# Overflow rows of a mixture-of-experts layer in blocks of 128 instead of 256

## The reference

```python
def _L0_ffn_ref(x, W1, b1, W2, b2, W3, b3, Wg, bg):
    gate_logits = jnp.einsum('bsd,dn->bsn', x, Wg) + bg
    gate_weights = jax.nn.softmax(gate_logits, axis=-1)
    topv, topi = jax.lax.top_k(gate_weights, TOPK)      # TOPK = 2, NE = 8
    h = gelu(einsum('bsd,ndh->nbsh', x, W1) + b1)        # 512 -> 1024
    h = gelu(einsum('nbsh,nhf->nbsf', h, W2) + b2)       # 1024 -> 1024
    eo = einsum('nbsf,nfd->nbsd', h, W3) + b3            # 1024 -> 512
    comb = jnp.sum(jax.nn.one_hot(topi, NE, dtype=x.dtype) * topv[..., None], axis=-2)
    return jnp.einsum('nbsd,bsn->bsd', eo, comb)
x = x + _L0_xattn_ref(_layernorm(x), ctx_2048, ...)
x = x + _L0_ffn_ref(_layernorm(x), ...)
```

## Time and profile before

| | us |
|---|---|
| median of three runs | 876.22 |
| lowest, highest | 872.66, 877.42 |
| the profiled execution | 865.58 |
| its span, first to last instruction | 863.8 |
| start of the first block's transposes | 419.88 |
| start of the ninth block's first matmul | 802.73 |
| end of its last matmul | 849.80 |
| last busy instruction (a scatter) ends | 855.18 |

### The profile page before, as it was taken

How to read it: one execution, slowest core, us unless ns; L and a number is a source line. 1 busy time by engine, 2 the same in 40 slices (tenths; PEclk the granted TensorE clock), 3 DMA queues, 4 the chain that set the end, 5 groups by cost and what they waited for, 6 DMA issues and landing times.

```text
span 863.8 us, 17380 instructions
## 1 busy us (share of the span) xinstructions
PE 775.2 (90%) x5934; PEld 672.6 (78%) x5934; DVE 601.8 (70%) x1275; ACT 495.6 (57%) x1131; POOL 231.1 (27%) x286
## 2 busy tenths in 40 slices
PE   3889898989998999766499999999999999999993
PEld 2657676767776767444498999999999999999992
DVE  4476878787979787655575858676766757676863
ACT  4357777777777767685153645554545455464551
POOL 3232434343434343213460303030211203030300
PEclk9799999999999999775699999999999999999997
DMA  6641010202020100222795655556465565565540
GB/s 212 242 151 58 2 59 20 72 23 69 23 69 28 65 22 24 84 108 93 256 341 202 242 213 207 214 196 232 176 260 204 216 225 210 203 246 203 206 169 2
DMA packets 28209, 126.22 MB, mean 146 GB/s; under 512 B 4236, under 2 KB 4252, under 8 KB 17664
## 3 DMA queue, kind: packets, MB, share of 16 engines
q1 hardware_dynamic: 22544, 109.80, 35.6%
q0 software_dynamic: 5616, 15.81, 5.2%
HBM read 108.68 MB, written 19.01 MB: 148 GB/s over the span
## 4 chain that ended last, share of the span: by engine, by line
PE 67%; DVE 12%; ACT 8%; issue 5%; DMA 3%; POOL 3%; SPq 0%; POOLq 0%; ACTq 0%; DVEq 0%
PE tiles L1041 6%; PE tiles L1043 6%; PE tiles L1042 6%; PE scores L1304 4%; PE scores L1305 4%; PE scores L1303 4%; PE ptb L1151 4%; PE pvb L1043 3%; PE pvb L1042 3%; PE pvb L1041 3%; PE ptb L1043 3%; PE ptb L1042 3%; PE ptb L1041 3%; PE scores L1141 2%; PE pvb L1174 2%
## 5 line engine op out<-in xcount | busy, mean ns | idle before, releaser
L830 DVE TENSOR_TENSOR w<-scr,w 128x2048 fp32r<-128x2048 f32 x75 | 170.8, 2288 | 61.6 <-ACT w L620 61.6
L620 ACT ACTIVATE w<-scr 128x2048 fp32r<-128x2048 f32 x76 | 144.9, 1909 | 60.8 <-PE scores L1305 60.8
L473 POOL DMA_INDIRECT out_dram<-scr,tok x18 | 19.4, 1079 | 311.4 <-DVE scr L1027 308.7
L602 ACT ACTIVATE scr<-scr,rsum 112x257 f32<-112x257 f32 x128 | 66.5, 520 | 62.4 <-DVE rsum L814 62.4
L1041 PE MATMUL tiles<-c,w 128*128 128x256 f32 (+1 forms) x272 | 82.4, 303 | 18.3 <-DVE c L718 15.7
L1041 PE MATMUL tiles<-w 128*128 128x256 f32 x288 | 83.3, 289 | 0.9 <-DVE w L1017 0.2
L1015 DVE CAST w<-scr 128x256 fp32r<-128x256 f32 x144 | 43.8, 304 | 54.6 <-ACT scr L686 54.6
L1042 PE MATMUL tiles<-w 128*128 128x256 f32 x288 | 81.5, 283 | 0.0
L1043 PE MATMUL tiles<-w 128*128 128x256 f32 x288 | 81.4, 283 | 0.0
L1151 PE MATMUL ptb<-ident,scr 112*128 112x112 f32 x384 | 64.7, 280 | 18.3 <-ACT scr L610 16.6
L1042 PE MATMUL tiles<-c,w 128*128 128x256 f32 (+1 forms) x272 | 79.4, 292 | 0.0
(11 more groups left out here) (214 smaller groups left out, 2315.1 us busy)
## 6 DMA issues: line engine op xcount, KB each, us to landing
scr<-in_dram SPq DMA_DIRECT2D x82, 1024.0 KB, 4.8
scr<-in_dram SPq DMA_DIRECT2D x8, 750.0 KB, 4.5
scr<-slots_d SPq DMA_DIRECT2D x10, 528.0 KB, 5.5
slots_d<-rows SPq DMA_DIRECT2D x8, 528.0 KB, 11.6
xn<-in_dram SPq DMA_DIRECT2D x9, 256.0 KB
xb<-in_dram SPq DMA_DIRECT2D x8, 224.0 KB, 2.6
xr<-in_dram SPq DMA_DIRECT2D x8, 224.0 KB, 2.5
out_dram<-x SPq DMA_DIRECT2D x8, 224.0 KB, 2.7
```

The lines of the kernel that those rows point to most:

```text
L602: act.activation(probs[0:L, s, 0:IMG], probs[0:L, s, 0:IMG], ACT.Copy, scale=rsum[0:L, g, s, 0:1]).then_inc(S["normal_img"], 1)
L620: act.activation(EH[slot], raw[slot], ACT.Copy).then_inc(S["eh_done"], 1)
L830: dve.tensor_tensor(EL[slot], raw[slot], EH[slot].bitcast(F32), ALU.subtract).then_inc(S["el_done"], 1)
```

## The change

`BLOCK` stays at 256, and `STEP` = 128 is new. The blocks 0 to 7 are now experts 0 to 7 with up to 256 rows each, without a condition: `Fori(0, E)` with the loop's own number as expert. What an expert has beyond 256 rows comes afterwards, in blocks of 128 rows, from `Fori(E, MAX_BLOCKS)` with the `If`. OVER = 5 is how many such blocks one expert can have, MAX_BLOCKS is now 18. The body of a block is a function on each engine, `expert_block`, written out for n = 256 and again for n = 128: a block of 128 rows has moving operands of 128 columns, one tile `t` instead of two, four transposes instead of eight for the block that follows it, one gather and one scatter. SyncE still loads 256 rows of `slots_d` for every block. The weights, all eight pieces, are loaded and converted for each block, of either size. On GpSimd the wait for the scatters (`added`) moves from the end of `add_block(j)` to the start of `add_block(j + 1)`, behind its wait for `xs_in`, and the conditional blocks are nested, so that the first one not needed skips all others.

```diff
 BLOCK = 256
-MAX_BLOCKS = (2 * T - E) // BLOCK + E
+STEP = P
+OVER = -(-(T - BLOCK) // STEP)
+MAX_BLOCKS = E + max(min(OVER * m, m + (2 * T - m * (BLOCK + 1)) // STEP) for m in range(1, 2 * T // (BLOCK + 1) + 1))
+ENTRIES = 24
...
             def add_block(j):
-                e = pool.value_load(ebi[0:1, j:j + 1], min_val=0, max_val=E - 1)
-
+                tiles_of = range(2 if j < E else 1)
+                rows_before = 2 * j if j < E else E + j
                 pool.wait_ge(S["xs_in"], 16 * (j + 1))
+                if j:
+
+                    pool.wait_ge(S["added"], 16 * rows_before)
...
-                for t in range(2):
+                for t in tiles_of:
...
-                pool.wait_ge(S["added"], 32 * (j + 1))
+            def add_overflow(j, used):
+
+                with pool.If(used > j):
+                    add_block(j)
+                    if j + 1 < MAX_BLOCKS:
+                        add_overflow(j + 1, used)
...
+                number = iota[:, 0:ENTRIES]
+                dve.tensor_scalar(over, number, float(E), None, ALU.subtract)
+                dve.scalar_tensor_tensor(main, number, float(E), number, ALU.is_lt, ALU.mult)
+                dve.tensor_scalar(rowf, number, float(STEP), float(BLOCK - E * STEP), ALU.mult, ALU.add).then_inc(S["table"], 1)
+                dve.wait_ge(S["table"], 1)
+                dve.scalar_tensor_tensor(blocks, number, float(E), rowf, ALU.is_ge, ALU.mult)
...
-            after(dve.tensor_scalar(nblk, nblk, 1.0, None, ALU.max))
...
+                                mm = three(hid[m % 4][:, 0:n], wh[:, c, i * P:(i + 1) * P], wl[:, c, i * P:(i + 1) * P],
+                                           vh[:, c, 0:n], vl[:, c, 0:n], c == 0, c == K - 1)
...
+                        if pc == 6:
+                            turn(j + 1, n)
...
+                            for t in range(n // P):
...
+            with pe.Fori(0, E) as j:
+                expert_block(j, BLOCK)
+            used = pe.value_load(ebi[0:1, MAX_BLOCKS + 1:MAX_BLOCKS + 2], min_val=E, max_val=MAX_BLOCKS)
+            with pe.Fori(E, MAX_BLOCKS) as j:
                 with pe.If(j < used):
+                    expert_block(j, STEP)
```

More of the change, by code:

```diff
@@ L469, in add_block @@
                     fill_overflow()
-                for t in range(2):
-                    pool.wait_ge(S["row_done"], 2 * j + t + 1)
+                for t in tiles_of:
+                    pool.wait_ge(S["row_done"], rows_before + t + 1)
                     pool.indirect_dma_start(
@@ L537, in _ @@
             pool.wait_ge(S["slots_done"], 1)
-            used = pool.value_load(ebi[0:1, MAX_BLOCKS + 1:MAX_BLOCKS + 2], min_val=1, max_val=MAX_BLOCKS)
-            for j in range(MAX_BLOCKS):
-                if j < E:
-                    add_block(j)
-                else:
-                    with pool.If(used > j):
-                        add_block(j)
+            used = pool.value_load(ebi[0:1, MAX_BLOCKS + 1:MAX_BLOCKS + 2], min_val=E, max_val=MAX_BLOCKS)
+            for j in range(E):
+                add_block(j)
+            add_overflow(E, used)
         @block.scalar
@@ L963, in _ @@
             gate_slots(LAST)
-            steps = [1]
+            steps = [2]
             def after(ins):
```

265 lines of the change are left out of this document (137 added, 128 removed).

## The result

| | median us | range of the runs |
|---|---|---|
| before | 874.46 | 872.66 to 877.42 |
| after | 859.78 | 856.78 to 866.80 |

The ratio of the two is 0.9846, with a 95% interval of 0.9812 to 0.9880. The forecast was 866.0 us, range 856 to 873, and faster with chance 0.80. The kernel became faster, and by more than forecast: 13.4 us by the ratio and 14.7 by the medians, where the working had 10.2.

What follows compares the result with a forecast made beforehand. TensorE's matmuls were taken to bound each expert block, at 47 us. Terms of 2.6 + 4.2 + 1.9 + 1.5 = 10.2 us came off the unprofiled median of 876.2, giving 866.0 us, range 856 to 873.

Steps and rivals of the forecast that it cites:

- hidden layers of the ninth block: 288 matmuls start every 0.111 us instead of 0.120, held by their weight loads; gain 2.6 us, bounds 0 and 15.6.
- output layer to the bias addition: Ninth block's output layer: half the transposes and wide matmuls go, VectorE's subtraction is then last; gain 4.2 us, bounds 3.5 and 5.9.
- bias addition to the last scatter: Ninth block's tail: the addition halves, the second weighting and second scatter go; gain 1.9 us, bounds 1.6 and 2.1.
- last scatter to the end: Program close: GpSimd no longer waits for the landing or steps over five empty blocks; gain 1.5 us, bounds 0 and 2.4.
- The first eight blocks: Blocks of 256 rows: matmuls, casts, transfers and order unchanged, so 0 us; they stay at 47 us.
- The step from the profiled execution to the median: Unprofiled median 876.2 us stood 10.6 above the profiled 865.6; the same gain was subtracted from it.
- minus 14: Largest gain in the forecast's own range: 876.2 minus 5.1 and minus 14 us, giving 862 to 871.
- rival of hidden loads: Ninth block's weight loads are no floor, spacing falls toward 0.066 to 0.08 us; gain 19 us, 857 us; chance 0.12.
- Loading new code: Ninth block's own code holds each engine 2 to 4 us at entry, gain stays small; 871 to 873 us; chance 0.09.
- The ninth block did fit into 128 rows: Rival: expert 7 has over 384 rows, a tenth block costs some 38 us more; held excluded, no chance given.

Runs made afterwards that it cites:

- e2: The changed kernel, unedited, run again; 861.37 us, ratio 0.9857 to the kernel before.
- e7: The changed kernel with SyncE loading the next rows behind the first weight piece instead of the fourth, in the 128-row body; 861.95 us, ratio 0.9843.
- e3: The kernel before with only GpSimd's wait for scatters moved and its conditional blocks nested; 872.8 us, ratio 0.9986.
- e5: The kernel before with 2 scatters of empty rows instead of 16; 857.73 us, ratio 0.9808.
- e6: The changed kernel with 2 scatters of empty rows instead of 16; 850.52 us, ratio 0.9702 to the kernel before.
- e8: The changed kernel with 64 columns instead of 128 in the hidden layers of the 128-row body; 886.48 us, ratio 1.0121 to the kernel before.
- e4: The changed kernel with STEP = 256, so blocks beyond 256 rows have 256 rows again; 869.61 us, ratio 0.9947 to the kernel before.
- e11: The changed kernel with STEP = 256 and register loads put back on SyncE ahead of the weight transfers; 858.34 us, ratio 0.9983 to the kernel before.
- e1: The kernel before, unedited, run again; 875.1 us, ratio 1.0021.
- third group: The runs of e9 to e12 on one chip with their own runs of the kernel before, which took 860.49 us.
- e9: The changed kernel with the 16 scatters of empty rows spread, two in each of the first eight blocks; 850.32 us, ratio 0.9865 to the kernel before.
- first two groups: The runs of e1 to e4 and of e5 to e8, each with its own runs of the kernel before: 874.07 and 876.33 us.
- e10: The changed kernel with the edits of e9 and e7 together; 850.04 us, ratio 0.9868 to the kernel before.
- e12: The changed kernel with 96 columns instead of 128 in the hidden layers of the 128-row body; 873.31 us, ratio 1.0163 to the kernel before.

## Why the prediction was right, point by point

| term | predicted us | measured us | where |
|---|---|---|---|
| hidden layers of the ninth block | 2.6 | 2.5 to 2.6 | e2, after |
| wait for unused rows | none | -0.7 to -1.0 | e2, after |
| output layer to the bias addition | 4.2 | 4.3 | e2, e7 |
| bias addition to the last scatter | 1.9 | 1.9 | after, e2 |
| last scatter to the end | 1.5 | 2.3 to 2.6 | e3, after, e2 |
| sum | 10.2 | 10.6 | e2; 10.7 between e5 and e6 |

**The hidden layers.** Right by its own reason: spacing 0.111 us, and from the first matmul's start to the last one's end 32.69 us (after) and 32.76 (e2) where 35.26 - 2.6 = 32.66 was worked out. e8 shows the floor directly, since 64 columns go no faster.

**The output layer.** Right: VectorE's subtraction for a weight piece that nobody uses is last, and the bias addition stands 7.63 us (e2) and 7.56 us (e7) behind the transposes, where 7.75 was forecast. The zero of that working, 837.99, is the end of the last hidden matmul; the transposes start at 837.83. Read from start to start throughout, e2 gains 2.5 in the hidden layers, loses 0.9 in the wait and gains 4.5 in the output layer, which is the same 6.1 us.

**What was missed in it.** The prediction followed the cover of the weight pieces, but not that of the next rows' load on SyncE's queue, which stands behind four waits for VectorE. It had at most 2 us of slack before (issued 5.7 us ahead of the transposes; such a load took 3.8 us to landing at the first block) and was late by 0.7 to 1.0 us after. Small, but it is a step left out: when TensorE's part shrinks, every transfer has to be asked whether it is late next.

**The last scatter to the end.** The mechanism was right and the term too small: the close is 6.0 to 6.2 us from GpSimd's last instruction, so the upper bound of 2.4 us was the value (wait 1.1, branches 1.25). The traces have up to 0.2 more, since the close is 6.2 us where the ninth block has two gathers and two scatters (e3, e4, e11) and 6.0 to 6.1 where it has one of each. The 1.5 was a middle between two readings where the earlier trace rows could not choose.

**The first eight blocks.** Seven of them took 328.5 and 329.2 us: nothing changed, as forecast. For the first the prediction had said that a block away from 47 us would prove it wrong, and the first trace had one. That was the hold-up, which e1 shows in the kernel before just as well. The prediction had taken the first block of its trace, 42.5 us, for the normal case, while the 876 us beside it came from executions with one of about 55.

**The step from the profiled execution to the median.** The 10.6 us between them were carried over unchanged, since "I know of nothing in the ninth block that this gap would change". That held, but without knowing what the gap was, and it was the step on which the 866.0 rested most. The gap is the hold-up's 13 us or so, less differences ahead of the experts. Had the changed kernel been timed without a hold-up, as before was in the third group, the same sum would have held and 866.0 would have been some 16 us too high (860.5 less 10.2 is 850.3).

**Why 859.8 and not 866.** The forecast had a range of its own, 862 to 871, and 859.8 lies below it (its "minus 14" is no sum of the bounds, which with 2.6 for the hidden layers come to 13.0); it is inside 856 to 873 only because that range was made wide enough for the rival of hidden loads at 857, which did not happen. So the cause was right, and that the number fell into the range was in part luck. Of the 6.2 us, 1.8 are before's median, which with a fourth run is 874.46 and not 876.22. Against before of the same group the changed kernel was 13.4 us (first), 12.5 (e2) and 13.8 us (e7) faster where before has the hold-up, and 11.6 us by the ratio, 10.2 by the medians (e9), where it has not. So about 10.5 us are the ninth block and the close, as the traces have it. What is above, 2 to 3 us, is hardly clear of noise: the intervals of e2 (10.2 to 14.8) and e9 (9.1 to 14.1) overlap, and only those of the first measurement (10.5 to 16.4) and e7 (11.6 to 15.9) lie at or above 10.5. e4, which has the static loop and 256 rows, may have them as well, with a first block 3 us shorter than e1's. The traces of e2 and e7 have first blocks of 53.2 and 53.1, but those of after and e8 have 55.6 and 55.9, no shorter than e1's, so the first blocks of single traces don't settle it. Whether there is such an excess, and whether the static loop makes it, is open.

**The rivals.** The loads did not hide (spacing 0.111, and 0.111 again at 64 columns). Loading new code cost nothing that the trace shows (0.23 us at the entry, in after and e4). The ninth block did fit into 128 rows.

**What stays open.** Why the engines are held in the burst at some times and not at others. The traces show that TensorE waits for no semaphore that they have, that it gets one to four matmuls through every 0.7 to 2.1 us, that this begins about 10 us after the first of the 16 scatters and ends within some 3 us of the last, and that e1 (held) and before (not held) are one program. ScalarE is held as well and earlier: in the seven traces with a hold-up its gelu of `ptb` starts 2.3 to 9.0 us after the last matmul of it, in the seven without 0.4. The loading of code doesn't explain it by what the traces show: in after the instruction queues move 16 KB at 426.5 us and nothing more until 453.1, so nothing while TensorE is held, and before has such a transfer at 431.2, within its burst, without being held. The state goes more by the time of the measurement than by the execution: all executions of before in the first two groups took 871.1 to 879.3 us and all in the third 857.1 to 865.1, and only at the first measurement did one of 865.6 stand beside four of 872.7 to 877.4. It is not the chip, since the first and third group were on the same one. What differs is not known.

## What to carry to other kernels

When a block's matmuls get narrower, count weight loads, not columns: below the width at which a matmul takes as long as the load of its weights, half of the columns buy almost nothing in it, and most of the gain (here 6 of the 8.7 us forecast) came from what is paid by wide matmuls and by the tail behind them. After such a cut, go through every transfer issued behind other waits on the same queue, for those with the least slack become waits. And before a difference between profiled and plain times is carried over, look at a second execution: here one and the same kernel spends 42 or 56 us in one block.

## What the runs showed of the hardware

- During a burst of 16 indirect scatters from GpSimd (each 128 rows of 528 numbers, 4.3 MB in 20 us) ScalarE and TensorE can be held up without a wait that the traces show: TensorE for some 10 us, with idle pieces of 0.2 to 1.8 us. Its clock falls to the lower level while this goes on and stays there for 13.7 us in after (433.1 to 446.8), 10.2 in e7. The first block then takes 53 to 56.5 us instead of 41 to 42.5. With 2 scatters (e5, e6) it did not show, in a group where kernels with 16 have it; spread over eight blocks (e9, e10) neither, but in a group without any hold-up.
- fp32r matmuls with a weight load of 128 columns each start every 0.111 us with 128 columns, and at the full clock also with 64 and 96; 256 columns take 0.120.
- TensorE's clock fell to 1.2 GHz in a stretch in which TensorE was busy all the time, in both kernels with thin matmuls, of 64 and of 96 columns beside weight loads of 128, and it stayed there for over 50 us. Being busy did not keep it up.
- The close of the program takes 6.0 to 6.2 us from the end of GpSimd's last instruction, whether or not its last scatter has landed. It depends on what GpSimd issued before: with 14 scatters fewer it is 1.2 us shorter (e6 against e2: 4.8 and 6.0), an estimate of 0.085 us for each.
- The best kernels are e9 and e10, 850.3 and 850.0 us, with all of the computation. They beat before (0.9865 [0.9836, 0.9894]); the changed kernel itself was not run in their group. That they also avoid the hold-up, worth some 10 us more where it comes (e6 850.5 against e7 862.0, less 1.2 for the close), is likely from e5 and e6 but was not measured in a group that had it.
